# Two units that project queries before values, small tables on ScalarE's DMA queue, and weight preparation spread over more units, in a fused two-layer attention kernel

## The chip, the cores and the metric

The kernel runs on one core of a Trainium2 chip. The metric is the device time of one execution in microseconds (us); a shorter time is better. The core's engines are named PE (TensorE, the matmuls), DVE (VectorE), ACT (ScalarE), POOL (GpSimd) and SP (SyncE, which issues most DMAs here). They run side by side and meet at semaphores only.

## What is computed

Two layers of the same form, one after the other, on x of 8 batches x 512 tokens x 512 features in float32. Layer 0 has 8 heads, layer 1 has 16. Cut from the reference:

```python
xn = _ln(x, ln_w, ln_b)
q = xn @ Wq + bq
k = xn @ Wk + bk + (1.0 - src_mask) * -1000000.0
q = jax.nn.softmax(q.reshape(b, t, h, dh), axis=-1)
k = jax.nn.softmax(k.reshape(b, t, h, dh), axis=1)
v = ((xn @ Wv + bv) * src_mask).reshape(b, t, h, dh)
att = jnp.einsum('bnhd,bnhl->bhdl', k, v)
y = jnp.einsum('bnhd,bhdl->bnhl', q, att).reshape(b, t, d)
emb_out = (jax.nn.silu(emb) @ W_emb + b_emb)[:, None, :]
scale, shift = jnp.split(emb_out, 2, axis=2)
hh = _ln(y, ln2_w, ln2_b) * (1.0 + scale) + shift
hh = jax.nn.silu(hh) @ W_out + b_out
return x + hh
```

So the attention is linear: K^T V is a 512x512 matrix, of which only the blocks of the heads count, and q multiplies it.

## The kernel before

**Units and steps.** A unit is one batch in one layer: units 0 to 7 are layer 0, units 8 to 15 are layer 1. Step u works on three units at once: the projections K, V, Q, the attention matrix (`att_ps`) and Y = q x attention (`attend`) of unit u ("front"); the transposition YT of the normalised Y, the scale-and-shift with silu (h) and the output projection O of unit u-1 ("back"); and the normalisation and transposition XT of unit u+1 ("following"). `step(u, front, back, following)` is written once for each engine; each engine runs its own list, and the lists meet at counting semaphores.

**Precision.** Every float32 operand is split in a high and a low float16 half, and a product is three matmuls (hi x hi, hi x lo, lo x hi; `split_pairs`, `product`, L417). One 128x512 tile of a projection is 12 matmuls. High halves are ACT's (`split_high`, L1031, L1081, L1132, L1063), low halves DVE's (`split_low` L720 for weights, L862 for K, L908 for q) or POOL's (L1182 for v, L1221 for h, L1177 for x).

**Weights.** The halves need a scale by the weight's largest entry. `find_peak` (L677) takes the peak of each row on DVE, PE sums over partitions (`sum_w`, L486), `find_scale` makes the power of two, and `split_high` and `split_low` follow. The order is K, V, Q, O. Layer 0's weights are prepared in the start and unit 0; those of layer 1 in units 1 to 4, one a unit, from the one buffer `w_stage` (`stages`), with the split in the unit behind. `gather_film` and `film_tables` make the scale-and-shift tables of a layer, at the end of unit 0 and in unit 8.

**PSUM.** The tiles of K, YT, V, Q, XT and O share a ring of six banks (Y takes O's). `slot` gives tile i of a stage its bank by its place in `SLOTS`, modulo six: K0 to K3 are in banks 0 to 3, YT0 to YT3 in 4, 5, 0, 1, V0 to V3 in 2, 3, 4, 5, Q0 to Q3 in 0, 1, 2, 3. `take_bank` lets PE wait until the tile that had the bank before, by `order(u)`, has been read; `FREES` names the semaphore: `k_masked` for K (DVE's read L836), `film_read` for YT (ACT's Identity L1102), `v_biased` for V (L894), `q_biased` for Q (L922).

**Order on the engines around the change.** PE in a step: K, YT, V, Q, attention, XT, O, attend. DVE: read K, statistics of the next x, h of blocks 0 and 1, low half of K, h of blocks 2 and 3, read V, peak of a weight (units 1 to 4), then for each tile of Q read, maximum and subtraction (L922, L925, L927), mask of the attention (L934), sums of q (L938), residual (L824), read Y (L964). ACT: normalised Y, exp of K, tanh and Identity of YT blocks 0 and 1 (L1095, L1102), high half of K, blocks 2 and 3, high half of h, of v, next x, exp and high half of q. SP: transposes k's and q's halves by DMA (L335) and issues the loads.

## Time and profile before

| | us |
|---|---|
| median of three runs | 897.56 |
| the three runs | 895.36 to 899.39 |
| the profiled execution | 897.69 |
| its span | 895.9 |

The span is the part of the execution that the hardware profiler covers; 1.8 us lie outside it. The mean clock granted to TensorE is 0.981 of full. The profile's page gives sums over the whole span, and its other views a stretch, an engine or a line. In a timeline a row is one instruction, or several alike in succession with their count; "[2.06 <-DMA ...]" says that the engine stood still for 2.06 us before it, and what ended that. Times start at the span's start. A matmul row's duration overlaps with the next; the distance of the starts is what counts.

### The profile page before, as it was taken

The numbers are of one execution on the slowest core, as the hardware profiler recorded it, in microseconds if no ns is written. First come the engines' busy times: TensorE is split into PE (matmuls) and PEld (weight loads), VectorE is DVE, ScalarE is ACT, GpSimd is POOL, SyncE is SP. The second block draws the span as 40 slices with busy tenths as digits, with TensorE's granted clock in tenths as the row PEclk, the third lists the DMA queues.
The fourth block names the chain that finished last, engine by engine and source line by source line (L and its number), as shares of the span: only waits on it lengthen the run. The fifth ranks groups of instructions, "written<-read, shape, count | busy, mean of one in ns | idle before, by whom it ended". The sixth has DMA issues, their size and how long they took to land.

```text
span 895.9 us, 13969 instructions
## 1 busy us (share of the span) xinstructions
PE 837.4 (93%) x5245; PEld 458.8 (51%) x5245; DVE 721.0 (80%) x1512; ACT 536.2 (60%) x913; POOL 382.2 (43%) x328
## 2 busy tenths in 40 slices
PE   3587999999999999999999899999999999999967
PEld 2236455454555446455554545555554645555544
DVE  5899897898888788787868978687786978687674
ACT  3456484857757594864827467474838567473713
POOL 1053355524545543453544236455534436455402
PEclk9897999999999999999999999999999999999988
DMA  9922135542526455231644224234443325223322
GB/s 317 352 47 49 59 48 108 141 106 44 142 63 142 106 154 141 56 86 60 193 102 95 61 68 110 69 95 106 94 106 92 86 48 112 66 48 95 48 48 94
DMA packets 162420, 90.83 MB, mean 101 GB/s; under 512 B 134673, under 2 KB 134961, under 8 KB 162353
## 3 DMA queue, kind: packets, MB, share of 16 engines
q1 hardware_dynamic: 162352, 89.94, 39.9%
q8 instruction: 41, 0.67, 0.3%
q14 instruction: 27, 0.21, 0.1%
HBM read 39.60 MB, written 16.78 MB: 63 GB/s over the span
## 4 chain that ended last, share of the span: by engine, by line
PE 53%; DVE 20%; issue 9%; ACT 9%; DMA 4%; POOL 4%; SPq 1%; DVEq 0%; POOLq 0%
PE ring L417 45%; PE ring L450 3%; PE att_ps L417 3%; DVE sb_v_or_q L922 2%; DVE sb_q_max L925 2%; DVE sb_kt_or_y L964 2%; DVE sb_y_stats L968 2%; ACT sb_k_or_qt L1073 2%; ACT sb_kq_hi L1081 2%; POOL sb_ht_lo L1221 2%; ACT sb_tanh L1095 1%; ACT sb_xh_or_h L1102 1%; DVE sb_row_peak L677 1%; DVE sb_tanh L908 1%; POOL sb_y_rstd L1172 1%
## 5 line engine op out<-in xcount | busy, mean ns | idle before, releaser
L417 PE MATMUL ring<-sb_w_hi,sb_xt_hi 128*128 128x512 f16 x512 | 194.6, 380 | 4.5 <-DVE sb_k_max L836 2.3
L417 PE MATMUL ring<-sb_w_hi,sb_xt_lo 128*128 128x512 f16 x512 | 194.8, 380 | 0.0
L417 PE MATMUL ring<-sb_w_lo,sb_xt_hi 128*128 128x512 f16 x512 | 194.6, 380 | 0.0
L1068 ACT ACTIVATE sb_kt_or_y<-sb_kt_or_y,sb_y_add,sb_y_rstd 128x512 f32<-128x512 f32 x64 | 46.9, 804 | 169.3 <-DVE sb_y_add L976 169.3
L1221 POOL TENSOR_TENSOR sb_ht_lo<-sb_xh_or_h,sb_ht_hi 128x512 f16<-128x512 f32 x60 | 68.5, 1170 | 114.3 <-ACT sb_ht_hi L1063 114.3
L417 PE MATMUL ring<-sb_xt_hi,sb_w_hi 128*128 128x512 f16 x256 | 97.9, 382 | 7.3 <-DVE sb_xt_lo L1005 7.3
L417 PE MATMUL ring<-sb_xt_lo,sb_w_hi 128*128 128x512 f16 x256 | 97.8, 382 | 0.0
L417 PE MATMUL ring<-sb_xt_hi,sb_w_lo 128*128 128x512 f16 x256 | 97.5, 381 | 0.0
L417 PE MATMUL ring<-sb_w_hi,sb_ht_hi 128*128 128x512 f16 x240 | 91.5, 381 | 5.1 <-ACT sb_xh_or_h L1053 4.4
L417 PE MATMUL ring<-sb_w_lo,sb_ht_hi 128*128 128x512 f16 x240 | 91.4, 381 | 0.0
L417 PE MATMUL ring<-sb_w_hi,sb_ht_lo 128*128 128x512 f16 x240 | 91.2, 380 | 0.0
L1128 ACT ACTIVATE sb_v_or_q<-sb_v_or_q 128x512 f32<-128x512 f32 x64 | 40.4, 631 | 80.1 <-DVE sb_v_or_q L927 80.1
L417 PEld LDWEIGHTS ring<-sb_w_hi,sb_xt_hi 128*128 128x128 f16 x512 | 50.2, 98 | 65.3 <-issue 3.9
L417 PEld LDWEIGHTS ring<-sb_w_hi,sb_xt_lo 128*128 128x128 f16 x512 | 50.2, 98 | 60.7 <-issue 0.6
L1191 POOL TENSOR_TENSOR sb_x<-sb_x,sb_bias_o 128x512 f32<-128x512 f32 x64 | 80.7, 1291 | 0.0
L1177 POOL TENSOR_TENSOR sb_xt_lo<-sb_xh_or_h,sb_xt_hi 128x512 f16<-128x512 f32 x60 | 67.5, 1156 | 30.4 <-ACT sb_xt_hi L1058 30.4
L417 PEld LDWEIGHTS ring<-sb_w_lo,sb_xt_hi 128*128 128x128 f16 x512 | 50.2, 98 | 58.4 <-issue 0.6
L1182 POOL TENSOR_TENSOR sb_v_parts<-sb_v_or_q,sb_v_parts 128x512 f16<-128x512 f32 x64 | 76.8, 1228 | 7.0 <-ACT sb_v_parts L1114 7.0
L1073 ACT ACTIVATE sb_k_or_qt<-sb_k_or_qt,sb_k_shift 128x512 f32<-128x512 f32 x64 | 45.4, 710 | 46.2 <-DVE sb_k_shift L844 46.2
L836 DVE CUSTOM_DVE_ANT_0 sb_k_or_qt<-ring,sb_mask_add,sb_scale_down 128x512 f32<-128x512 f32 x64 | 46.4, 744 | 32.6 <-issue 32.5
L1186 POOL TENSOR_TENSOR sb_att_lo<-sb_att,sb_att_hi 128x512 f16<-128x512 f32 x16 | 18.5, 1158 | 121.1 <-ACT sb_att_hi L1134 121.1
L922 DVE SCALAR_TENSOR_TENSOR sb_v_or_q<-ring,sb_scale_down,sb_bias_q 128x512 f32<-128x512 f32 x64 | 47.6, 744 | 20.9 <-POOL sb_v_parts L1182 20.8
(184 smaller groups left out, 1764.0 us busy)
## 6 DMA issues: line engine op xcount, KB each, us to landing
out<-sb_x SPq DMA_DIRECT2D x15, 1024.0 KB, 5.1
sb_x<-out SPq DMA_DIRECT2D x8, 1024.0 KB, 5.9
sb_x<-in_x SPq DMA_DIRECT2D x7, 1024.0 KB, 10.1
sb_mask_raw<-in_mask SPq DMA_DIRECT2D x16, 256.0 KB, 6.0
sb_w_stage<-in_L_cond_Wk SPq DMA_DIRECT2D x2, 1024.0 KB, 6.9
sb_w_hi<-in_L_cond_W_emb SPq DMA_DIRECT2D x2, 1024.0 KB, 11.7
sb_w_lo<-in_L_cond_W_emb SPq DMA_DIRECT2D x2, 1024.0 KB, 12.5
sb_wemb<-in_L_cond_film_emb_W SPq DMA_DIRECT2D x2, 1024.0 KB, 6.5
```

The costliest lines, as they stand in the source:

```text
L417: last = nc.tensor.matmul(out, lhs, rhs, start=(n == 0), stop=(n == len(pairs) - 1))
L450: last = nc.tensor.transpose(out[:, j * P:j * P + P], source(i, j), ident[:])
L836: nc.vector.tensor_tensor_reduce(k_or_qt[:, i, :], bank("K", i), mask_add[:], scale_down[:, front, K_:K_ + 1], -3.4e38, ALU.add, ALU.max, ...
L922: nc.vector.scalar_tensor_tensor(out=q[:, t, :], in0=bank("Q", t), scalar=scale_down[:, front, Q_:Q_ + 1], in1=bias_q[front][:], op0=ALU.m ...
L1068: nc.scalar.activation(kt_or_y[:, t, :], kt_or_y[:, t, :], ACT.Identity, bias=y_add[:, t:t + 1], scale=y_rstd[:, t:t + 1]).then_inc(yh_rea ...
L1073: nc.scalar.activation(k_or_qt[:, i, :], k_or_qt[:, i, :], ACT.Exp, bias=k_shift[:, i:i + 1], accum_out=k_sum[:, i:i + 1]).then_inc(k_exp, 1)
L1128: nc.scalar.activation(q[:, t, :], q[:, t, :], ACT.Exp).then_inc(q_exp, 1)
L1177: nc.gpsimd.tensor_tensor(xt_lo[:, c, :], xh_or_h[:, c, :], xt_hi[:, c, :], ALU.subtract).then_inc(xt_lo_ready, 1)
L1182: nc.gpsimd.tensor_tensor(v_lo[:, t, :], v[:, t, :], v_hi[:, t, :], ALU.subtract).then_inc(v_lo_ready, 1)
L1186: nc.gpsimd.tensor_tensor(att_lo[:], att[:], att_hi[:], ALU.subtract).then_inc(att_lo_ready, 1)
L1191: nc.gpsimd.tensor_tensor(xt(unit, t), xt(unit, t), bias_o[layer][:], ALU.add).then_inc(x_biased, 1)
L1221: nc.gpsimd.tensor_tensor(lo[:, c, :], xh_or_h[:, c, :], hi[:, c, :], ALU.subtract).then_inc(ht_lo_ready, 1)
```

## The change

Six pieces:

1. `QUERIES_FIRST`: in units 0 and 15 the projection of Q stands in front of V. q then has the buffer `wemb` instead of `v_or_q`. Banks by `slot` stay as they are.
2. The five small tables (column table, identity, embedding, mask, head blocks) are issued by ACT instead of SP. The transposition of the mask on PE and its copy stand behind K's weight preparation.
3. Layer 0's weights are prepared in the order K, Q, V, O (`NTH`). W_v and W_q change buffers.
4. Unit 0: DVE reads and centres all of q in front of k's low half and `v_scales`, and `gather_film`, the peak of W_o and the scales of layer 1's norm stand in front of the reads of Y. XT and the film transposition stand in front of the attention on PE. The halves of W_o are made in unit 1.
5. Layer 1's weights: W_q is loaded in `wemb` between steps 0 and 1, W_k in unit 1 behind k's transposed low half, W_v in unit 3, W_o in unit 4. Peaks stand in units 1 to 4 (K, Q, V, O), scales and high halves in units 2 to 5, low halves in units 3 to 6. The film weights are loaded in units 6 and 7. In unit 8 `gather_film` stands in front of the last read of K, and `film_tables` in front of q.
6. Unit 15: Q, V, then two tiles of O in front of the attention. DVE reads q0 and q1 in front of k's low half, q2 and q3 behind it, and centres all four behind h.

```diff
+QUERIES_FIRST = (0, UNITS - 1)
+NTH = (0, 2, 1, 3)
...
-    here = [(name, i) for name, i in SLOTS if 0 <= u + OFFSET[name] < UNITS]
+    stages = [name for name, _ in STAGES]
+    if u in QUERIES_FIRST:
+        v, q = stages.index("V"), stages.index("Q")
+        stages[v], stages[q] = "Q", "V"
...
-        stages = ((w_stage, kt_or_y, v_parts, w_stage), (w_stage,) * 4)
+        stages = ((w_stage, v_parts, kt_or_y, w_stage), (w_stage, w_stage, wemb, wemb))
...
                 turn(kt_hi, kq_hi[:], k_hi_ready, 4 * (u + 1), kt_hi_ready)
-                if 2 <= u <= 4:
-                    load_w(1, u - 1)
+                if u in (3, 4):
+                    load_w(1, (V_, O_)[u - 3])
                 turn(kt_lo, k_lo, k_lo_ready, 4 * (u + 1), kt_lo_ready)
...
+                if u == 1:
+                    load_w(1, K_)
...
+                if u not in QUERIES_FIRST:
+                    values()
...
                 project_tokens("Q", u, Q_, front, xt_hi, xt_lo, between=with_q)
+                if u in QUERIES_FIRST:
+                    values()
+                if u == 0:
+                    turn_x(u)
+                    turn_film(0)
+                if u == UNITS - 1:
+                    pe.wait_ge(ht_lo_ready, 4 * u)
+                    project_tokens("O", u, O_, back, ht_hi, ht_lo, (0, 1))
...
                 if u_is_first:
+                    split_low(0, V_)
+                    x_affine(u + 1)
+                    for t in range(T):
+                        read_q(t)
+                        centre_q(t)
                     split_k()
+                    v_scales(0)
...
+                        if c == 2 and u == UNITS - 1:
+                            read_q(0)
+                            read_q(1)
                         if c == 2 and front is not None:
                             split_k()
+                        if c == 2 and u == UNITS - 1:
+                            read_q(2)
+                            read_q(3)
...
                 if u_is_first:
                     gather_film(0)
+                    find_peak(0, O_)
+                    ln_scales(1)
...
+                if u == 1:
+                    split_high(0, O_)
...
-                    elif u == B:
-                        gather_film(1)
+                    elif u == B:
+                        film_tables(1)
+                        output_scale(1)
...
+            act.dma_start(cols[:], cols_d).then_inc(cols_loaded, 16)
+            act.dma_start(ident[:], ident_d).then_inc(ident_loaded, 16)
+            act.dma_start(emb, emb_d).then_inc(emb_loaded, 16)
+            act.dma_start(mask_rows, mask0_d.rearrange("b (t p) -> (b t) p", p=P)).then_inc(mask_rows_loaded, 16)
+            act.dma_start(blocks[:], blocks_d).then_inc(tables_loaded, 16)
```

**PE, unit 15, from the YT transposes on.** L450 and L461 are the transposes, L417 and L428 the matmuls of a product; ring0 to ring5 are the six banks. Before, then after:

```order
L450 MATMUL ring0<-sb_ident,sb_kt_or_y 128x128 [waits k_masked]
L450 MATMUL ring0<-sb_ident,sb_kt_or_y 128x128 x3
L450 MATMUL ring1<-sb_ident,sb_kt_or_y 128x128 [waits k_masked]
L450 MATMUL ring1<-sb_ident,sb_kt_or_y 128x128 x3
L417 MATMUL ring2<-sb_w_hi4,sb_xt_hi 128x512 [waits k_masked]
```

```order
L461 MATMUL ring0<-sb_ident,sb_kt_or_y 128x128 [waits k_masked]
L461 MATMUL ring0<-sb_ident,sb_kt_or_y 128x128 x3
L461 MATMUL ring1<-sb_ident,sb_kt_or_y 128x128 [waits k_masked]
L461 MATMUL ring1<-sb_ident,sb_kt_or_y 128x128 x3
L428 MATMUL ring0<-sb_w_hi4,sb_xt_hi 128x512 [waits film_read]
```

The first projection behind the transposes has moved from bank 2 (V0, where K2 was) to bank 0 (Q0, where YT2 is), and its wait from DVE's read of K to ACT's read of YT.

**DVE, unit 15, from the reciprocal of k's sums on.** L882 and L961 are h, L862 and L885 k's low half, L894 and L892 the reads of V, L922 and L902 the reads of Q, L925 and L907 the maximum, L927 and L909 the subtraction. Before, then after:

```order
L851 RECIPROCAL sb_k_recip<-sb_k_sum 128x4 [waits k_sum_scaled]
L882 SCALAR_TENSOR_TENSOR sb_xh_or_h<-sb_tanh,sb_xh_or_h 128x512 [waits film_read] x2
L862 SCALAR_TENSOR_TENSOR sb_k_or_qt<-sb_k_or_qt,sb_k_recip,sb_kq_hi 128x512 [waits k_hi_ready,k_recip_ready]
L862 SCALAR_TENSOR_TENSOR sb_k_or_qt<-sb_k_or_qt,sb_k_recip,sb_kq_hi 128x512 [waits k_lo_ready,k_hi_ready] x3
L882 SCALAR_TENSOR_TENSOR sb_xh_or_h<-sb_tanh,sb_xh_or_h 128x512 [waits film_read] x2
L894 SCALAR_TENSOR_TENSOR sb_v_or_q<-ring,sb_scale_down,sb_bias_v 128x512 [waits pe_V] x4
L922 SCALAR_TENSOR_TENSOR sb_v_or_q<-ring,sb_scale_down,sb_bias_q 128x512 [waits pe_Q,v_lo_ready]
```

```order
L872 RECIPROCAL sb_k_recip<-sb_k_sum 128x4 [waits k_sum_scaled]
L961 SCALAR_TENSOR_TENSOR sb_xh_or_h<-sb_tanh,sb_xh_or_h 128x512 [waits film_read] x2
L902 SCALAR_TENSOR_TENSOR sb_wemb<-ring,sb_scale_down,sb_bias_q 128x512 [waits pe_Q] x2
L885 SCALAR_TENSOR_TENSOR sb_k_or_qt<-sb_k_or_qt,sb_k_recip,sb_kq_hi 128x512 [waits k_hi_ready,k_recip_ready]
L885 SCALAR_TENSOR_TENSOR sb_k_or_qt<-sb_k_or_qt,sb_k_recip,sb_kq_hi 128x512 [waits k_lo_ready,k_hi_ready] x3
L902 SCALAR_TENSOR_TENSOR sb_wemb<-ring,sb_scale_down,sb_bias_q 128x512 [waits pe_Q] x2
L961 SCALAR_TENSOR_TENSOR sb_xh_or_h<-sb_tanh,sb_xh_or_h 128x512 [waits film_read] x2
L907 TENSOR_REDUCE sb_q_max<-sb_wemb 128x16 [waits q_biased]
```

The reads of Q have moved in front of and right behind k's low half, and no longer wait for v's low half; the reads of V stand behind the centring of q.

**SP, from q's transposes of unit 0 into unit 1.** L335 and L350 are the DMA transposes, L311 and L326 the loads of weights, L302 and L314 the load of the next mask. Before, then after:

```order
L335 DMA_TRANSPOSE sb_k_or_qt<-sb_tanh 128x16x128 [waits q_lo_ready]
L311 DMA sb_w_stage<-in_L_cond_Wk 128x4x512 [waits w_ready0]
L302 DMA sb_mask_raw<-in_mask 128x512 [waits mask_ready]
L335 DMA_TRANSPOSE sb_kt_or_y<-sb_kq_hi 128x16x128 [waits pe_YT,k_hi_ready]
L335 DMA_TRANSPOSE sb_kt_or_y<-sb_k_or_qt 128x16x128 [waits k_lo_ready]
```

```order
L350 DMA_TRANSPOSE sb_k_or_qt<-sb_tanh 128x16x128 [waits q_lo_ready]
L326 DMA sb_wemb<-in_L_cond_Wq 128x4x512 [waits q_lo_ready,q_summed]
L314 DMA sb_mask_raw<-in_mask 128x512 [waits mask_ready]
L350 DMA_TRANSPOSE sb_kt_or_y<-sb_kq_hi 128x16x128 [waits pe_YT,k_hi_ready]
L350 DMA_TRANSPOSE sb_kt_or_y<-sb_k_or_qt 128x16x128 [waits k_lo_ready]
L326 DMA sb_w_stage<-in_L_cond_Wk 128x4x512 [waits w_ready0]
```

The load of layer 1's W_k has moved from in front of unit 1's transposes to behind them; W_q of layer 1 has its old place.

## Rows read from the trace of the kernel before

**Rows 1.** The page, busy time of each engine over the whole span

```profile
PE 837.4 (93%) x5245; PEld 458.8 (51%) x5245; DVE 721.0 (80%) x1512; ACT 536.2 (60%) x913; POOL 382.2 (43%) x328
```

**Rows 2.** Timeline of PE, first attend product, units 0, 1, 2, 4; start, duration

```profile
84.79 0.26 PE L417 MATMUL ring<-sb_att_hi,sb_k_or_qt 128*128 128x128 f16 x1 [5.37 <-DMA sb_k_or_qt<-sb_tanh]
...
142.22 0.22 PE L417 MATMUL ring<-sb_att_hi,sb_k_or_qt 128*128 128x128 f16 x1 [0.89 <-issue]
...
195.46 0.22 PE L417 MATMUL ring<-sb_att_hi,sb_k_or_qt 128*128 128x128 f16 x1 [0.36 <-issue]
...
300.25 0.22 PE L417 MATMUL ring<-sb_att_hi,sb_k_or_qt 128*128 128x128 f16 x1 [0.40 <-issue]
```

**Rows 3.** Timeline of PE, start of the attention products, units 10 and 11

```profile
597.27 0.89 PE L417 MATMUL att_ps<-sb_kt_or_y,sb_v_parts 128*128 128x128 f16 x13
...
647.58 0.61 PE L417 MATMUL att_ps<-sb_kt_or_y,sb_v_parts 128*128 128x128 f16 x8
```

**Rows 4.** Line 311 between 8 and 9 us, the load of W_v

```profile
L311 SPq DMA_DIRECT2D sb_kt_or_y<-in_L_cond_Wv x1: 650/650/650, 8.4 to 8.4; - x1
...
DMA to landing us min/median/max: 11.8/11.8/11.8
```

**Rows 5.** Timeline of DVE, the start: peak of W_v

```profile
21.02 2.28 DVE L677 TENSOR_REDUCE sb_row_peak<-sb_kt_or_y 128x4 f32<-128x2048 f32 x1
```

**Rows 6.** Timeline of PE, unit 0: first matmuls of K, first of V

```profile
29.18 0.61 PE L417 MATMUL ring<-sb_xt_hi,sb_w_hi 128*128 128x512 f16 x1 [7.34 <-DVE sb_xt_lo L1005]
29.58 0.63 PE L417 MATMUL ring<-sb_xt_lo,sb_w_hi 128*128 128x512 f16 x1
...
44.19 0.38 PE L417 MATMUL ring<-sb_w_hi,sb_xt_hi 128*128 128x512 f16 x1 [2.31 <-DVE sb_k_max L836]
```

**Rows 7.** Timeline of DVE: reads of Y, low half of W_o, read of K

```profile
86.84 1.39 DVE L964 TENSOR_TENSOR sb_kt_or_y<-ring,sb_q_recip 128x512 f32<-128x512 f32 x2
...
99.21 2.08 DVE L720 SCALAR_TENSOR_TENSOR sb_w_lo<-sb_w_stage,sb_scale_up,sb_w_hi 128x512 f16<-128x512 f32 x3
...
101.96 0.74 DVE L836 CUSTOM_DVE_ANT_0 sb_k_or_qt<-ring,sb_mask_add,sb_scale_down 128x512 f32<-128x512 f32 x1
```

**Rows 8.** Timeline of SP, unit 1: transposition of k's low half

```profile
114.91 3.32 SPq L335 DMA_TRANSPOSE sb_kt_or_y<-sb_k_or_qt  x1
```

**Rows 9.** Line 311 between 166 and 168 us, a load beside a transposition

```profile
DMA to landing us min/median/max: 6.9/6.9/6.9
```

**Rows 10.** Timeline of DVE: first read of q in units 1, 2, 5; unit 2's peak

```profile
122.38 0.75 DVE L922 SCALAR_TENSOR_TENSOR sb_v_or_q<-ring,sb_scale_down,sb_bias_q 128x512 f32<-128x512 f32 x1
...
173.60 2.29 DVE L677 TENSOR_REDUCE sb_row_peak<-sb_w_stage 128x4 f32<-128x2048 f32 x1 [2.06 <-DMA sb_w_stage<-in_L_cond_Wv]
...
177.43 0.75 DVE L922 SCALAR_TENSOR_TENSOR sb_v_or_q<-ring,sb_scale_down,sb_bias_q 128x512 f32<-128x512 f32 x1
...
331.83 0.75 DVE L922 SCALAR_TENSOR_TENSOR sb_v_or_q<-ring,sb_scale_down,sb_bias_q 128x512 f32<-128x512 f32 x1 [2.25 <-POOL sb_v_parts L1182]
```

**Rows 11.** Timeline of PE, unit 8: first attend product

```profile
512.80 0.23 PE L417 MATMUL ring<-sb_att_hi,sb_k_or_qt 128*128 128x128 f16 x1 [1.45 <-DVE sb_x L824]
```

**Rows 12.** Timeline of PE, unit 15: V, attention, attend

```profile
828.28 0.38 PE L417 MATMUL ring<-sb_w_hi,sb_xt_hi 128*128 128x512 f16 x1
...
849.00 1.17 PE L417 MATMUL att_ps<-sb_kt_or_y,sb_v_parts 128*128 128x128 f16 x18
...
863.46 0.26 PE L417 MATMUL ring<-sb_att_hi,sb_k_or_qt 128*128 128x128 f16 x1 [3.85 <-DMA sb_k_or_qt<-sb_tanh]
```

**Rows 13.** Timeline of ACT, unit 15: Identity of YT block 2

```profile
836.53 0.77 ACT L1102 ACTIVATE sb_xh_or_h<-ring,sb_film_now 128x512 f32<-128x512 f32 x1
```

**Rows 14.** Timeline of POOL, unit 15: low half of v

```profile
843.68 4.94 POOL L1182 TENSOR_TENSOR sb_v_parts<-sb_v_or_q,sb_v_parts 128x512 f16<-128x512 f32 x4
```

**Rows 15.** Timeline of DVE, unit 15: sums of q, residuals, first read of Y

```profile
857.11 2.46 DVE L938 TENSOR_REDUCE sb_q_sum<-sb_v_or_q 128x16 f32<-128x512 f32 x4
...
860.36 1.97 DVE L824 SCALAR_TENSOR_TENSOR sb_x<-ring,sb_down_o,sb_x 128x512 f32<-128x512 f32 x3
...
865.00 0.69 DVE L964 TENSOR_TENSOR sb_kt_or_y<-ring,sb_q_recip 128x512 f32<-128x512 f32 x1 [2.67 <-PE ring L417]
```

More of the change, by code:

```diff
@@ L499, in sum_ln @@
                 for layer in range(LAYERS):
-                    last = nc.tensor.matmul(sums[0][:, 8 + layer:9 + layer], ones[:], peak[:, layer, LN:LN + 1], start=True, stop=True)
+                    last = nc.tensor.matmul(sums(0, 8 + layer), ones[:], peak[:, layer, LN:LN + 1], start=True, stop=True)
                 last.then_inc(ln_summed, 1)
@@ new lines, in step, with read_q @@
+                q = queries(u)
+                if front is not None:
+                    by_head = lambda a: a.rearrange("p (h e) -> p h e", h=heads)
+                    wide = lambda a: a.unsqueeze(2).broadcast_to([P, heads, D // heads])
+                def read_q(t):
+                    dve.wait_ge(done["Q"], 4 * u + t + 1)
+                    nc.vector.scalar_tensor_tensor(out=q[:, t, :], in0=bank("Q", t), scalar=scale_down[:, front, Q_:Q_ + 1],
+                                                   in1=bias_q[front][:], op0=ALU.mult, op1=ALU.add).then_inc(q_biased, 1)
@@ L1105, in step, with split_v @@
                         high(c)
-                if front is not None:
+                q = queries(u)
+                def split_v():
                     if front == 0:
```

282 lines of the change are left out of this document (151 added, 131 removed).

## Prediction, made before the changed kernel was run

> **What bounds the kernel now.** I read the page first. TensorE is busy 93% of the span [rows 1], so only its gaps, and its stretches at a lowered clock, can move the end. The next view is the timeline of TensorE at the same point of every unit. Between units 10 and 11 the attention products lie 50.31 us apart (647.58 - 597.27) with nothing but matmuls between them [rows 3]: that is the dense unit. The first attend products of units 0, 1, 2 and 4 lie farther apart: 142.22 - 84.79 = 57.4, then 53.24, then 104.79 for two units [rows 2]. So the slack is at both ends: the start until unit 4 (the units 2 to 4 alone are 53.24 + 104.79 - 3 x 50.31 = 7.1 over dense; the weights of layer 1 are measured there), unit 8, and the last unit with the chain behind it. The timelines of VectorE, ScalarE, GpSimd and SyncE at those places say what TensorE waits for.
>
> **Start, part by part.** K of unit 0 starts at 29.18, behind VectorE [rows 6]. VectorE is occupied in one piece from 21.02: peak of W_v, low half of W_k, low half of x^T [rows 5], 8.16 us. The change puts W_q there in place of W_v. Its two V-only steps go (0.4), and VectorE reaches it earlier, because the wait for the mask transposition is gone; then the landing of W_q decides. W_v, second in the queue, was issued at 8.42 and landed 11.8 later, at 20.2 [rows 4]. W_q takes this place with five small issues gone ahead of it; the DMA engines are full all this time, so I gain little of them: 19.9. K starts at 19.9 + 7.8 = 27.7, 1.5 earlier (bounds: 0, were W_q late, to 3).
>
> Here the Trainium skill has a rule that speaks against part of the change: "DMA: Bandwidth & Descriptors", section "Issuing engines are not separate DMA queues", says that transfers issued from ScalarE and SyncE share the same 16 engines, so a second issuing engine brings no bandwidth. The trace of before has one issuing engine only and can't show it; 11.8 us for 1 MB agrees with engines that are full. By the rule the tables' move gives only the issue time on SyncE; were it wrong, W_q would land up to 2 us sooner.
>
> The wait of 2.31 in front of V [rows 6] goes: before, the reads of K, whose bank V takes, stood on VectorE behind v_scales; this stands after q now, and the reads begin at 36. That makes 3.8 us by the time of attention in unit 0, and attend starts earlier still, near 77 to 79 against 84.79, since q is centred before attention. But behind attend VectorE now has gather_film, the peak of W_o (2.28 and 0.3 of small steps, by the peak in [rows 5]) and the scales of the second layer norm (1.3) ahead of the reads of Y. I walk VectorE through its new order with the old durations: the reads of K end at 41, q is read and centred until 56, k's low half stands at 59.5, v's scales at 62.1, v is read until 64.8. GpSimd's low half of v ends 4.6 behind that read, as before; so attention products at 69.4, sums of q done 76.1, gather_film until 81, peak 83.6, scales 84.9. Y is read at 84.9 instead of 86.84 [rows 7]. From there to the read of K of unit 1 at 101.96 stand the same steps less the low half of W_o, 4 x 0.69 = 2.7 [rows 7], plus its scale, 0.9. So K of unit 1 is read at 98.3; with 0.3 for meeting GpSimd, 98.6, **3.4 earlier** (0.5 to 5).
>
> **Unit 1.** The low half of W_o moves behind k_recip, where VectorE waits for ScalarE anyway: 0.3. Before, K^T's low half was issued at 114.91, 12.95 after K was read, and took SyncE 3.32 [rows 8]. Now it is issued at 98.6 + 12.95 + 0.3 = 111.85 and done at 115.2. W_k of layer 1 is loaded only behind it; before, it was in place long before it was needed. Such a load landed, beside a transposition, in 6.9 [rows 9]. With no other transfer in flight I take 0.8 less, an estimate between 5 and 6.9; so 121.3. Its peak stands in VectorE's order ahead of the first read of Q, takes 2.6, and puts that read at 123.9 instead of 122.38 [rows 10]. What is queued behind this wait is all of q, and attend waits for that. In unit 2 attend came 195.46 - 177.43 = 18.0 after the same read [rows 2, 10]. So attend of unit 1 starts at 141.95, against 142.22: of 3.4 us **0.3 are left** (with the landing and K's read at their ends, -2.5 to +2).
>
> **Units 2 to 4.** Unit 2 now measures W_q, loaded long before into wemb: no wait of 2.06 [rows 10], and the peak nearly fits in the 2.25 that VectorE waits there for v's low half in an undisturbed unit [rows 10]. So 50.4 instead of 53.24. Unit 3 has W_v instead of W_q, whose steps from the peak on take 177.43 - 173.60 = 3.83 on VectorE [rows 10] against 2.6: 1.25 lost; unit 4 has W_o as before. Together **1.6 gained** (0 to 3). The high and low halves, now a unit later, stand where ScalarE and VectorE wait; film loads had no wait before and have none now: 0.
>
> **Unit 8.** Film tables stood between the residuals, and attend waited 1.45 for them [rows 11]. They now stand ahead of q, in place of gather_film, which stands ahead of the last read of K. **1.5 gained** (0 to 3: nothing if the gather makes K late, twice the stall if the clock and q gain too).
>
> **Unit 15.** This is the term that decides. Before, V follows the YT transposes at once, at 828.28, since its bank 2 was K's and long read [rows 12]. Q first means bank 0, and bank 0 is YT2's. ScalarE frees it with the Identity of feature block 2, which starts at 836.53 and takes 0.77 [rows 13], behind the high halves of K. Nothing of the change makes this earlier. So TensorE stands still from 828.28 to 837.3, 9.0 us, and restarts at half clock: in unit 0, after 7.34 of standing still, nine matmuls went at a distance of 0.40 to 0.43 [rows 6], where V's and Q's 96 took 849.00 - 828.28 = 20.7 [rows 12], 0.216 each. That is 1.9 more. Q ends at 849.6, V at 860.0. Two output tiles fill 860.0 to 865.2. V's low half on GpSimd took 4.94 for four [rows 14]; it starts at 861.1, after ScalarE's exp and high halves of q, and ends at 866.0. Attention products 2.9: 868.9; masking 0.7; sums of q 2.46 and 0.8 [rows 15]: 872.9; three residuals 1.97 [rows 15]: Y is read from 874.9 instead of 865.00 [rows 15]. Before, TensorE entered attend after 3.85 of standing still [rows 12] and VectorE waited a further 0.5 between two Y; that is gone. 874.9 - 865.0 - 0.5: **9.4 lost** (6 to 11). Behind it the chain to the end is the same.
>
> **Sum.** -0.3 - 1.6 - 1.5 + 9.4 = +6.0. The profiled execution took 897.69 with a span of 895.9; 897.69 + 6.0 = 903.7. The median of 897.56 is 0.1 below the profiled one, so this isn't corrected. A difference under 0.5%, 4.5 us, can't be told from none for this kernel: its bounds are 893.1 and 902.05.
>
> **Rivals.**
> The tail costs TensorE's own work only (0.24; work as above, but v's low half is ready when V and the output tiles end, for ScalarE is through with q early). Then O and attention end at 870.8, Y is read from 871.5, and 6.0 is lost. Against it speaks that high halves of q stand ahead of v on ScalarE. 897.69 - 3.4 + 6.0 = 900.3. To it belongs that attend of unit 1 keeps the 3.4 us (W_k lands before v's low half is ready): 897.69 - 6.5 + 9.4 = 900.6.
>
> Faster (0.08): the bank of YT2 is free early, or Q starts on another bank. It decides if Q starts within 3 us of 828.28. Then q's transposes are landed long before attend, the wait of 3.85 goes, and 3.4 + 3.85 are gained: 890.4. For it: early q is what the wait of 3.85 asks for. Against it: the timeline of ScalarE.
>
> Start worse (0.16): the order of unit 0 on VectorE meets GpSimd's work, W_k lands at 6.9 or later, and the gather makes K of unit 8 late. No gain of 3.4 and up to 1.5 lost, tail 9.3 to 10.5: 907 to 909.
>
> The start's tables change nothing (within my own case, 0.52): K starts at 29.18; this takes 1.5 from the read of K, and 905.
>
> **How the numbers follow.** The likeliest, 0.52, gives 903.7, with its own range 901 to 906; a fourth of it lies under 902.05. Same: 0.12 of it, 0.21 of the first rival, 0.02 beside: 0.35. Slower: 0.40, 0.15 and 0.02: 0.57. Faster: 0.08. The range of 898 to 909 leaves out the fast rival, and about 0.08 of others.
>
> **What would show it.** Right: TensorE idle some 9 us in front of Q of unit 15, ended by the Identity on ScalarE; a lowered clock after it; v's low half as the releaser of attention there; Y read 9 to 10 us later, counted from the YT transposes. W_k's load as the releaser of VectorE's peak in unit 1. The wait ahead of V in unit 0 gone, attend of unit 2 some 50.4 behind that of unit 1, no wait of attend for x in unit 8. Wrong: Q of unit 15 close behind the transposes; or unit 1's first attend earlier than 140.

## The result, and the profile after

The changed kernel is slower: a median of 908.03 us in four executions (907.64 to 908.43), against 898.47 for the kernel before in its four (895.36 to 899.5). The ratio is 1.0112, with a 95% interval of 1.0085 to 1.0138. The forecast was 903.7 with a range of 898 to 909, so the direction and the range held and the size was missed by 4.3 us. The time lies outside the 901 to 906 that the likeliest case had for itself. The profiled execution took 907.77, its span 906.0, and its mean granted clock is 0.977 of full (0.981 before).

The page of the kernel after, busy time of each engine (against [rows 1]):

```profile
PE 842.1 (93%) x5245; PEld 460.9 (51%) x5245; DVE 718.2 (79%) x1510; ACT 536.2 (59%) x915; POOL 386.1 (43%) x328
```

No engine has less or more to do in any way that matters: the same 5245 matmuls, and VectorE 2.8 us less busy. TensorE's span grew by 10.1: 4.7 of it is busy time (842.1 against 837.4 for the same matmuls, at a lower mean clock), and 5.4 is gaps (63.9 against 58.5). The waits of TensorE, grouped by what ended them (us in total, times, longest), show the new ones:

```profile
PE ring L428 <- ACT sb_xh_or_h L1151: 8.9, 1, 8.9
...
PE att_ps L428 <- POOL sb_v_parts L1260: 4.1, 2, 2.2
PE ring L428 <- DVE sb_wemb L902: 3.1, 1, 3.1
PE ring L428 <- POOL sb_att_lo L1264: 2.9, 1, 2.9
...
PE ring L428 <- DVE sb_x L841: 2.1, 1, 2.1
```

The first is the bank of YT2 in unit 15; the second and fourth stand at the attention of units 0 and 15; the third is V's first tile in unit 0, behind a read of Q; the last is attend of unit 15, behind the residuals.

**The start.** Timelines of VectorE, TensorE and GpSimd, unit 0 of the kernel after, in order of time:

```profile
18.62 2.29 DVE L699 TENSOR_REDUCE sb_row_peak<-sb_kt_or_y 128x4 f32<-128x2048 f32 x1 [0.40 <-DMA sb_kt_or_y<-in_L_cond_Wq]
...
26.40 0.61 PE L428 MATMUL ring<-sb_xt_hi,sb_w_hi 128*128 128x512 f16 x1 [4.50 <-DVE sb_xt_lo L1051]
...
43.84 4.75 DVE L742 SCALAR_TENSOR_TENSOR sb_w_lo<-sb_v_parts,sb_scale_up,sb_w_hi 128x512 f16<-128x512 f32 x4
...
44.65 6.30 POOL L1269 TENSOR_TENSOR sb_x<-sb_x,sb_bias_o 128x512 f32<-128x512 f32 x4
...
54.76 0.58 PE L428 MATMUL ring<-sb_w_hi,sb_xt_hi 128*128 128x512 f16 x1 [3.09 <-DVE sb_wemb L902]
...
66.70 5.85 POOL L1260 TENSOR_TENSOR sb_v_parts<-sb_v_or_q,sb_v_parts 128x512 f16<-128x512 f32 x4 [15.76 <-ACT sb_v_parts L1165]
...
67.63 5.47 DVE L914 SCALAR_TENSOR_TENSOR sb_tanh<-sb_wemb,sb_kq_hi 128x512 f16<-128x512 f32 x4
...
72.81 5.28 PE L428 MATMUL att_ps<-sb_v_parts,sb_kt_or_y 128*128 128x128 f16 x48 [1.94 <-POOL sb_v_parts L1260]
...
78.12 0.69 DVE L930 TENSOR_TENSOR sb_att<-att_ps,sb_blocks 128x512 f32<-128x512 f32 x1 [5.03 <-PE att_ps L428]
```

Two rows of the kernel before, on VectorE and TensorE, stand against these:

```profile
49.36 6.72 DVE L862 SCALAR_TENSOR_TENSOR sb_k_or_qt<-sb_k_or_qt,sb_k_recip,sb_kq_hi 128x512 f16<-128x512 f32 x4 [0.86 <-ACT sb_kq_hi L1081]
...
73.13 2.84 PE L417 MATMUL att_ps<-sb_v_parts,sb_kt_or_y 128*128 128x128 f16 x48
```

K starts 2.8 earlier than before (26.40 against 29.18 [rows 6]), but the attention only 0.3 earlier (72.81 against 73.13). In between, low halves on VectorE and work on GpSimd stand side by side twice and both are slow, and V waits for Q. Before had one such meeting too: k's low half took 6.72 beside GpSimd's 6.30 for x and its bias, and takes 3.31 in after, where GpSimd is idle. The attention itself then takes 5.28 where the same 48 matmuls took 2.84. Y of unit 0 is read at 87.60, behind 86.84 of before [rows 7], and K of unit 1 at 100.66, against 101.96.

**Unit 1.** SyncE's queue, VectorE's peak of W_k, and the first product of attend (against 142.22 in [rows 2]):

```profile
114.39 3.06 SPq L350 DMA_TRANSPOSE sb_kt_or_y<-sb_k_or_qt  x1
117.51 0.58 SPq L326 DMA_DIRECT2D sb_w_stage<-in_L_cond_Wk  x1
...
123.47 2.29 DVE L699 TENSOR_REDUCE sb_row_peak<-sb_w_stage 128x4 f32<-128x2048 f32 x1 [4.69 <-DMA sb_w_stage<-in_L_cond_Wk]
...
145.41 0.22 PE L428 MATMUL ring<-sb_att_hi,sb_k_or_qt 128*128 128x128 f16 x1 [1.67 <-issue]
```

Attend of unit 1 is 3.2 later than before, behind a load for which VectorE stands still 4.69 us.

**Unit 15.** Timelines of TensorE, GpSimd and VectorE (against [rows 12, 14, 15]):

```profile
826.01 1.91 PE L461 MATMUL ring<-sb_ident,sb_kt_or_y 128*128 128x128 f32 x16
836.83 0.61 PE L428 MATMUL ring<-sb_w_hi,sb_xt_hi 128*128 128x512 f16 x1 [8.91 <-ACT sb_xh_or_h L1151]
...
859.75 5.37 DVE L914 SCALAR_TENSOR_TENSOR sb_tanh<-sb_wemb,sb_kq_hi 128x512 f16<-128x512 f32 x4
...
860.05 6.08 POOL L1260 TENSOR_TENSOR sb_v_parts<-sb_v_or_q,sb_v_parts 128x512 f16<-128x512 f32 x4 [6.52 <-ACT sb_v_parts L1171]
...
866.41 4.47 PE L428 MATMUL att_ps<-sb_kt_or_y,sb_v_parts 128*128 128x128 f16 x48 [2.19 <-POOL sb_v_parts L1260]
...
875.58 0.22 PE L428 MATMUL ring<-sb_att_hi,sb_k_or_qt 128*128 128x128 f16 x1 [2.10 <-DVE sb_x L841]
...
876.66 1.28 DVE L1011 TENSOR_TENSOR sb_kt_or_y<-ring,sb_q_recip 128x512 f32<-128x512 f32 x2
```

From the YT transposes to the first read of Y it takes 876.66 - 826.01 = 50.65; before, it took 38.47 (its transposes start at 826.53, just ahead of [rows 12]). That distance is the measure of unit 15 in all runs below. A stretch's table, for the attention products of units 15 and 0 (us, PE busy, granted clock, DMA share, GB/s), shows why they are long: 0.50 of full, the 1.2 GHz level, for all of unit 0's and the later part of unit 15's.

```profile
868.00:870.00 2.00, 2.00 (x22) 0.50 0.51 94
72.80:78.10 5.30, 5.28 (x48) 0.50 0.52 99
```

### The profile page after: what moved, and what is told of

Its sections match the earlier page's. It is cut to its first block, busy times and chain, and to the rows that moved or that the text cites. A ratio compares the mean times of both kernels' runs of the same rounds, so it can differ in the third digit from the quotient of the medians.

```text
span 906.0 us, 13953 instructions
## 1 busy us (share of the span) xinstructions
PE 842.1 (93%) x5245; PEld 460.9 (51%) x5245; DVE 718.2 (79%) x1510; ACT 536.2 (59%) x915; POOL 386.1 (43%) x328
## 4 chain that ended last, share of the span: by engine, by line
PE 59%; DVE 18%; issue 7%; ACT 7%; DMA 4%; POOL 3%; SPq 1%; DVEq 0%; POOLq 0%; ACTq 0%
PE ring L428 50%; PE att_ps L428 4%; PE ring L461 3%; DVE sb_q_max L907 2%; DVE sb_v_or_q L902 2%; DMA sb_kt_or_y<-in_L_cond_Wq 2%; DVE sb_row_peak L699 2%; DVE sb_w_lo L742 1%; ACT sb_k_or_qt L1122 1%; POOL sb_v_parts L1260 1%; ACT sb_kq_hi L1130 1%; DVE sb_kt_or_y L1011 1%; ACT sb_tanh L1144 1%; DVE sb_y_stats L1015 1%; ACT sb_xh_or_h L1151 1%
## 5 line engine op out<-in xcount | busy, mean ns | idle before, releaser
L428 PE MATMUL ring<-sb_w_hi,sb_xt_hi 128*128 128x512 f16 x512 | 195.9, 383 | 12.0 <-ACT sb_xh_or_h L1151 8.9
L428 PE MATMUL ring<-sb_w_lo,sb_xt_hi 128*128 128x512 f16 x512 | 195.7, 382 | 0.0
L428 PE MATMUL ring<-sb_w_hi,sb_xt_lo 128*128 128x512 f16 x512 | 195.6, 382 | 0.0
L428 PE MATMUL ring<-sb_xt_hi,sb_w_hi 128*128 128x512 f16 x256 | 98.0, 383 | 4.7 <-DVE sb_xt_lo L1051 4.5
L428 PE MATMUL ring<-sb_xt_lo,sb_w_hi 128*128 128x512 f16 x256 | 97.8, 382 | 0.0
L428 PE MATMUL ring<-sb_xt_hi,sb_w_lo 128*128 128x512 f16 x256 | 97.8, 382 | 0.0
L428 PE MATMUL ring<-sb_w_hi,sb_ht_hi 128*128 128x512 f16 x240 | 91.0, 379 | 7.2 <-ACT sb_xh_or_h L1100 4.5
L428 PE MATMUL ring<-sb_w_lo,sb_ht_hi 128*128 128x512 f16 x240 | 91.0, 379 | 0.0
L428 PE MATMUL ring<-sb_w_hi,sb_ht_lo 128*128 128x512 f16 x240 | 91.0, 379 | 0.0
L1260 POOL TENSOR_TENSOR sb_v_parts<-sb_v_or_q,sb_v_parts 128x512 f16<-128x512 f32 x64 | 79.3, 1270 | 22.3 <-ACT sb_v_parts L1165 15.8
L428 PEld LDWEIGHTS ring<-sb_w_hi,sb_xt_hi 128*128 128x128 f16 x512 | 50.5, 99 | 72.9 <-ACT sb_xh_or_h L1151 9.1
L428 PEld LDWEIGHTS ring<-sb_w_hi,sb_xt_lo 128*128 128x128 f16 x512 | 50.4, 99 | 61.6 <-issue 2.1
L428 PEld LDWEIGHTS ring<-sb_w_lo,sb_xt_hi 128*128 128x128 f16 x512 | 50.5, 99 | 59.4 <-issue 1.7
L1176 ACT ACTIVATE sb_v_or_q<-sb_v_or_q 128x512 f32<-128x512 f32 x56 | 35.4, 632 | 70.0 <-DVE sb_v_or_q L909 70.0
L961 DVE SCALAR_TENSOR_TENSOR sb_xh_or_h<-sb_tanh,sb_xh_or_h 128x512 f32<-128x512 f32 x64 | 45.4, 724 | 20.3 <-ACT sb_xh_or_h L1151 20.2
```

The costliest lines, as they stand in the source:

```text
L428: last = nc.tensor.matmul(out, lhs, rhs, start=(n == 0), stop=(n == len(pairs) - 1))
L961: nc.vector.scalar_tensor_tensor(out=xh_or_h[:, c, :], in0=tanh[:, c % 2, :], scalar=1.0, in1=xh_or_h[:, c, :], op0=ALU.add, op1=ALU.mult) ...
L1176: nc.scalar.activation(q[:, t, :], q[:, t, :], ACT.Exp).then_inc(q_exp, 1)
L1260: nc.gpsimd.tensor_tensor(v_lo[:, t, :], v[:, t, :], v_hi[:, t, :], ALU.subtract).then_inc(v_lo_ready, 1)
```

## The experiments

All times are medians, with the ratio to the kernel before as run on the same chip (its medians there: 897.31 for the first four, 898.83 for the next three and the first of "Together", 898.68 for the rest). "After" is the changed kernel, 908.03. Where two runs stem from different chips, their ratios are compared, and a difference of about 0.1% between them isn't clear of noise.

### Which part loses: unit 15 in its old order

```diff
-QUERIES_FIRST = (0, UNITS - 1)
+QUERIES_FIRST = (0,)
```

and with it the places of the two output tiles, of the reads of Q and of ACT's q and v in unit 15, as before.

> The changed kernel, with unit 15 in its old order (K, YT, V, Q, attention, O) on all engines; everything else of the change stays. Theory (the loss is unit 15's): the 8.9 us of TensorE in front of Q and what follows it go, attend of unit 15 falls from 875.6 to about 863.2, and the time is 908.0 - 10.4 = 897.6, the kernel before's within 1 us. Rival (part of the loss is the start: W_k of layer 1 late, q's low halves beside GpSimd): over 901.

Measured: 896.34 (894.84 to 899.6), ratio 0.9989, 0.9973 to 1.0006. YT to Y takes 38.50 again. The whole loss, 11.7 us against after, is unit 15's; the rest of the change together is worth about nothing.

### Is it the bank: Q of unit 15 in V's banks

```diff
 def slot(name, i, u=None):
+    if u in OTHER_BANKS:            # (UNITS - 1,)
+        name = {"V": "Q", "Q": "V"}.get(name, name)
     return 3 if name == "O'" else slot("O", i) if name == "Y" else SLOTS.index((name, i)) % RING
```

The order of the work is that of after. Only the banks differ in unit 15: Q takes 2 to 5, V takes 0 to 3.

> The changed kernel with Q first in unit 15, but Q in banks 2, 3, 4, 5 and V in 0, 1, 2, 3 of the ring in that unit, so that Q0's bank is K2's, long read. Theory (the bank of YT2 is what Q waits for): TensorE has no gap of 8.9 behind the YT transposes, Q starts within 1 us of them, and v's low half ends near 856.5 instead of 866.1; VectorE reads Y near 867.5 instead of 876.7; 908.0 - 9 = 899. Rival 1 (early q saves the wait of 3.85 ahead of attend, once the bank is free): 893 or less. Rival 2 (Q waits for something else too): the gap stays, 907 to 908.

Measured: 898.65 (896.95 to 901.76), ratio 1.0012, 0.9995 to 1.0028. The 8.9 us are gone, and TensorE runs through. The profiled execution was the longest of the ten, 901.76, so distances within the unit are compared here, not times from the start. Its timeline from the transposes on, GpSimd's low half of v, and the attention:

```profile
829.06 1.91 PE L466 MATMUL ring<-sb_ident,sb_kt_or_y 128*128 128x128 f32 x16
830.81 0.38 PE L433 MATMUL ring<-sb_w_hi,sb_xt_hi 128*128 128x512 f16 x1
...
854.12 6.06 POOL L1265 TENSOR_TENSOR sb_v_parts<-sb_v_or_q,sb_v_parts 128x512 f16<-128x512 f32 x4 [6.52 <-ACT sb_v_parts L1176]
...
860.43 4.47 PE L433 MATMUL att_ps<-sb_kt_or_y,sb_v_parts 128*128 128x128 f16 x48 [2.18 <-POOL sb_v_parts L1265]
...
869.59 0.22 PE L433 MATMUL ring<-sb_att_hi,sb_k_or_qt 128*128 128x128 f16 x1 [2.10 <-DVE sb_x L846]
```

YT to Y takes 870.67 - 829.06 = 41.61: 9.0 less than after, but 3.1 more than in the old order. So the bank explains most of the loss, and the rival "faster" had its mechanism right and its price wrong. With Q in time, v is what comes late: its low half, then a half-clock attention, then the sums of q and the residuals, for which attend still waits 2.10.

### Unit 1: W_k loaded ahead of k's transposes

```diff
+                if u == 1:
+                    load_w(1, K_)
                 turn(kt_hi, kq_hi[:], k_hi_ready, 4 * (u + 1), kt_hi_ready)
...
-                if u == 1:
-                    load_w(1, K_)
```

> The changed kernel with the load of layer 1's W_k in unit 1 in front of k's transposed high half instead of behind the low half. Theory (the load's landing holds q of unit 1): issued near 110, landed near 116, VectorE's wait of 4.69 ahead of the peak is gone, q is first read at 121.5 instead of 126.1, attend of unit 1 starts near 141 instead of 145.4, and all units behind keep it: 908.0 - 4.5 = 903.5. Rival (the two transpositions get slower beside the load and attention waits for them, or ScalarE holds q): 1.5 or less gained, 906.5 or more.

Measured: 904.49 (902.95 to 905.17), ratio 1.007, 1.0046 to 1.0094; 3.5 less than after. VectorE's first read of q stands at 121.38 instead of 126.07, and attend at

```profile
141.38 0.22 PE L428 MATMUL ring<-sb_att_hi,sb_k_or_qt 128*128 128x128 f16 x1 [1.04 <-issue]
```

instead of 145.41. The load behind the low half costs these 4.0 us, of which 3.4 are left at the YT transposes of unit 15 (822.57 against 826.01).

### Unit 0: V and Q with swapped banks

The edit of the second experiment, for unit 0 instead of unit 15.

> The changed kernel with V and Q in each other's banks in unit 0 alone, so that V0 doesn't wait for the read of Q2. Theory (VectorE's order bounds unit 0, TensorE's wait of 3.09 is covered): the wait goes, attention starts under 1 us earlier than 72.8, K of unit 1 is read under 1 us earlier than 100.7: 907.0 to 908.0, the same as the changed kernel. Rival (V's late start is what makes v's low half and attention late): the 3.09 and 1.5 of half clock come back, attention at 68.5, and 904 to 905.

Measured: 909.84 (908.26 to 910.1), ratio 1.0129, 1.0108 to 1.015. The 3.09 in front of V are gone and no time is won; the 1.8 more than after aren't clear of noise (the intervals overlap), though the forecast was at most 908. TensorE arrives early and then waits: 1.83 for a read of v in front of XT, 0.77 for the film's pick, and 4.20 for GpSimd in front of the attention, which starts at 73.76:

```profile
65.18 1.31 PE L466 MATMUL ring<-sb_ident,sb_xh_or_h 128*128 128x128 f32 x8 [1.83 <-DVE sb_v_or_q L897]
67.14 6.37 POOL L1265 TENSOR_TENSOR sb_v_parts<-sb_v_or_q,sb_v_parts 128x512 f16<-128x512 f32 x4 [15.75 <-ACT sb_v_parts L1170]
```

So unit 0 is bounded by the order on VectorE and GpSimd, not by this wait. (XT's wait for v's reads, 0.41 in after, grows with the swap, so the run doesn't test a unit 0 without any wait for a bank.) A wait that tops the list needn't be the one that counts.

### The sums of q ahead of the mask

In after, VectorE stands idle 5.0 and 5.8 us in front of the masking of the attention, and sums q behind it. In units 0 and 15:

```diff
                     for t in range(T):
                         low_q(t)
+                    sum_q()
                     mask_att()
-                    sum_q()
```

> The changed kernel with the sums of q and their reciprocal (3.25 us on VectorE) in front of the mask of the attention instead of behind it, in units 0 and 15. VectorE stands still there for 5.0 and 5.8 us until the attention products end. Theory (behind these products the end waits for VectorE's order): in unit 15 the residuals start at 871.6 instead of 874.8, attend's wait of 2.1 for x goes, Y is read near 874, 2.6 earlier; in unit 0 the reads of Y move by 3.2, K of unit 1 with them, and the load of W_k too, so 2.5 to 3 are kept: 908.0 - 5.5 = 902.5. Rival (W_k or another transfer swallows unit 0's part): 905.5. Rival 2 (TensorE and GpSimd's half of the attention are the bound): 907 to 908.

Measured: 904.18 (903.11 to 905.4), ratio 1.0068, 1.0049 to 1.0088. YT to Y takes 48.08, 2.6 less, and attend of unit 1 comes at 143.04, 2.4 earlier. That is between the theory (902.5) and its rival (905.5). And 1.6 of the tail's 2.6 is the clock: here the attention of unit 15 took 2.84 behind a wait of 2.16, where after had 4.47 behind 2.19.

### The sums also ahead of q's low half

```diff
+                    dve.wait_ge(q_exp, 4 * (u + 1))
+                    sum_q()
                     for t in range(T):
                         low_q(t)
-                    sum_q()
                     mask_att()
```

The sums read one operand, the low halves two. So VectorE has one-operand work while GpSimd makes v's low half.

> As the run with the sums early, but the sums of q stand in front of q's low halves too. The low halves (5.4 us for four beside GpSimd's low half of v, 2.75 alone) then meet v's low half only at its end. Theory (both engines slow each other when both read two operands): v's low half takes 5.0 to 5.4 instead of 5.9 to 6.1, attention of unit 15 starts 0.8 earlier, the low halves take 3 to 4; but q's transposed low half is issued 2 later, near 867, and attend of unit 15 starts near 873.5: within 1 us of the run with the sums early, 902 to 903.5. Rival (the two don't meet): v's low half stays at 6, and the later transposition makes it 904 or more.

Measured: 901.67 (899.75 to 903.21), ratio 1.0033, 1.002 to 1.0047. Timelines of VectorE, GpSimd and TensorE, unit 15:

```profile
857.90 2.46 DVE L920 TENSOR_REDUCE sb_q_sum<-sb_wemb 128x16 f32<-128x512 f32 x4
...
858.20 4.49 POOL L1261 TENSOR_TENSOR sb_v_parts<-sb_v_or_q,sb_v_parts 128x512 f16<-128x512 f32 x4 [6.53 <-ACT sb_v_parts L1172]
...
862.14 2.91 DVE L914 SCALAR_TENSOR_TENSOR sb_tanh<-sb_wemb,sb_kq_hi 128x512 f16<-128x512 f32 x4
...
862.95 2.84 PE L428 MATMUL att_ps<-sb_kt_or_y,sb_v_parts 128*128 128x128 f16 x48 [0.58 <-POOL sb_v_parts L1261]
```

The same four GpSimd instructions take 4.49 instead of 6.08, the same four on VectorE 2.91 instead of 5.37. Nothing differs but what stands beside them: the slowness in after is the meeting of the two. Attend now waits for the transposition of q's low half (1.12) and no longer for the residuals. YT to Y is 46.41.

### The kernel before, with the tables and unit 8's film alone

The five small loads move from SP to ACT, and in unit 8 `gather_film` and `film_tables` take the places that after gives them. The mask's transposition and everything else stay as before.

```diff
-            sp.dma_start(ident[:], ident_d).then_inc(ident_loaded, 16)
...
+            act.dma_start(cols[:], cols_d).then_inc(cols_loaded, 16)
+            act.dma_start(ident[:], ident_d).then_inc(ident_loaded, 16)
...
+                        if u == B and i == C - 1:
+                            gather_film(1)
```

> The kernel before with two parts of the change alone: the five small tables issued by ScalarE, and unit 8's film work moved (gather in front of the last read of K, tables in front of q). Units 0 and 15, and all weights, in their old order. Theory (tables: SyncE's issue time and W_v's landing; film: a stall of 1.45): K of unit 0 starts near 27.5 instead of 29.2, but the reads of K there still stand behind v_scales, and attention waits for the same chain on VectorE, so 1.5 of it arrives at unit 1; unit 8's attend has no wait for x: 897.3 - 3 = 894.5. Rival (both are hidden): 897.3. The mask's transposition stays in front here, so that the start may gain nothing: then 895.8.

Measured: 894.37 (890.54 to 897.53), ratio 0.9952, 0.9935 to 0.9968. TensorE at K's and V's first tile of unit 0, and attend of unit 1:

```profile
26.85 0.61 PE L411 MATMUL ring<-sb_xt_hi,sb_w_hi 128*128 128x512 f16 x1 [6.62 <-DVE sb_xt_lo L999]
41.99 0.38 PE L411 MATMUL ring<-sb_w_hi,sb_xt_hi 128*128 128x512 f16 x1 [2.31 <-DVE sb_k_max L832]
...
140.22 0.22 PE L411 MATMUL ring<-sb_att_hi,sb_k_or_qt 128*128 128x128 f16 x1 [1.13 <-issue]
```

K starts nearly as early as in after, V's wait of 2.31 is still there, and K of unit 1 is read at 99.71, 0.9 earlier than in after. So the tables alone bring most of the earlier start. From K's start to the read of K of unit 1 it takes 72.9, as before (72.8), against 74.3 in after: queries first in unit 0, with what was moved along with it there, loses 1.5. The profiled execution is the shortest of the ten, 3.8 under the median. Part of that lies in the tail: the last attend ran at full clock and took 2.6, where before's took 5.2 at 0.50.

### The tables back on SP

On the kernel of the first experiment, the five loads go back to SP, to the places that before gives them.

> The changed kernel with unit 15 in its old order and the five tables issued by SyncE again, in their old places. Theory (the start's gain is the tables'): the scales of the norm wait for the column table and embedding again, W_q lands later, K of unit 0 starts at 27.5 to 29 instead of 26.4, and unit 1 follows: 896.3 + 2 = 898.3. Rival (the reordered preparation made the gain, the mask's transposition being gone from the front): K starts at 26.5 to 27 and 896.3 to 896.8.

Measured: 897.76 (896.49 to 901.36), ratio 0.9997, 0.9983 to 1.0012. With the tables on ACT the ratio was 0.9989, and the two intervals overlap, so the medians alone don't show a gain. SyncE's issue of W_q with the tables on ACT (the first experiment) and here, then VectorE's peak of W_q and the first matmul of K here:

```profile
4.20 1.34 SPq L326 DMA_DIRECT2D sb_kt_or_y<-in_L_cond_Wq  x1
...
8.08 0.46 SPq L326 DMA_DIRECT2D sb_kt_or_y<-in_L_cond_Wq  x1
...
19.82 2.29 DVE L700 TENSOR_REDUCE sb_row_peak<-sb_kt_or_y 128x4 f32<-128x2048 f32 x1 [1.66 <-DMA sb_kt_or_y<-in_L_cond_Wq]
...
27.60 0.61 PE L434 MATMUL ring<-sb_xt_hi,sb_w_hi 128*128 128x512 f16 x1 [4.23 <-DVE sb_xt_lo L1043]
```

With the tables on ACT the same peak started at 18.39, and K at 26.16: W_q was issued 3.9 sooner and landed 1.4 sooner. In all the runs with the start of after, K starts between 25.99 and 27.07, so the move is worth 0.5 to 1.6 us at K's start. The new order of the preparation brings something by itself too: K starts at 27.60 here against 29.18 before, with the tables on SP in both.

### Together, unit 15 in the old order

The first and third experiments, and in unit 0 the sums of q, the peak of W_o and the scales of layer 1's norm ahead of the mask.

> The changed kernel with unit 15 in its old order, W_k's load in front of k's transposes in unit 1, and in unit 0 the sums of q, the peak of W_o and the scales of layer 1's norm in front of the mask of the attention. Theory (the three losses add up): 896.3 by the run with unit 15 undone, less 3.5 to 4 for W_k, less 3 to 5 for VectorE's 5 us of standing still in unit 0: 888 to 890, about 1% below the kernel before. Rival (what unit 0 gains is taken back by TensorE's half clock or the film tables before unit 1): 892 to 893.

Measured: 888.71 (888.46 to 890.87), ratio 0.9897, 0.9878 to 0.9916. Attend of unit 1 comes at 137.36.

The same with `sum_q` ahead of `low_q` in unit 0:

> The merged kernel (unit 15 in its old order, W_k early, peak of W_o and scales of the norm ahead of the mask) with the sums of q also ahead of q's low halves in unit 0. Theory (low halves of q and of v slow each other): v's low half from about 5.6 to 4.6, attention of unit 0 starts 0.5 to 1 earlier, and K of unit 1 with it: 888.0. Rival (unit 0 is held by the peak of W_o in front of the mask): the same 888.7.

Measured: 889.12 (888.66 to 889.64), ratio 0.9895, 0.988 to 0.991: no difference in the time. In the profiled executions there is one until the tail: attention of unit 0 starts at 71.55 instead of 72.96, though masking then waits for the peak of W_o and the scales of the norm, which end at 77.56; attend of unit 1 comes at 136.42 instead of 137.36, and the YT transposes of unit 15 at 817.43 instead of 818.51. The last attend then takes 5.2 at 0.50 of the clock, where the other's took 4.3, and the spans are 886.8 and 886.9. So 1.1 was won in unit 0 and most of it was lost again to the clock at the end.

### Queries first in unit 15 after all

The kernel just above, but with unit 15 as in after, Q and V in swapped banks there, and the sums ahead of q's low half.

> The same, but unit 15 in the change's order with Q first, with Q and V in each other's banks, and the sums ahead of q's low halves there too. From the YT transposes to the first read of Y: 38.5 us in the old order, 50.7 in the changed kernel, 41.6 with other banks, 46.4 with the sums first. Theory (both gains add up): 41.6 - 4.2 = 37.4, 1 us less than in the old order, 887.0. Rival (with the bank free, v's low half is the bound, and the sums can't help since VectorE reads v late): 40 to 41, 890 to 891.

Measured: 886.11 (885.4 to 887.68), ratio 0.9864, 0.9846 to 0.9882: the fastest kernel of the study, 1.4% under the kernel before. The start of attend of unit 15 in the kernel just above and here, and the first read of Y here:

```profile
854.39 0.27 PE L428 MATMUL ring<-sb_att_hi,sb_k_or_qt 128*128 128x128 f16 x1 [3.88 <-DMA sb_k_or_qt<-sb_tanh]
...
853.18 0.22 PE L433 MATMUL ring<-sb_att_hi,sb_k_or_qt 128*128 128x128 f16 x1 [0.50 <-DMA sb_k_or_qt<-sb_tanh]
...
854.12 1.29 DVE L1018 TENSOR_TENSOR sb_kt_or_y<-ring,sb_q_recip 128x512 f32<-128x512 f32 x2 [0.65 <-PE ring L433]
```

The YT transposes start at 816.98, so it takes 37.14, 1.4 less than the 38.50 of the old order. The four reads of Y then follow each other in 3.0 us (854.12 to 857.12), where with Q last they need 3.8 (855.93 to 859.70). Attend waits 0.50 for the transposed q instead of 3.88, and runs at full clock, 2.8 us, instead of 5.2 at 0.50. Projecting queries first in the last unit is a gain of 3.0 us (886.11 against 889.12), once it has banks that are free and an order on VectorE that meets GpSimd less (v's low half takes 4.95). The clock is a good part of it: the old order too can have its last attend at full clock (2.6 in the seventh experiment), and from the first read of Y to the end it then took 29.3, against 29.6 here and 30.9 in the kernel just above.

## Why the prediction was right, and where it was off

**Unit 15 (right, slightly under).** TensorE's standstill was forecast at 9.0 and measured 8.91, ended by ScalarE's Identity as said; the restart at half clock is there, shorter than forecast (six matmuls 0.40 to 0.43 apart, 836.83 to 839.36, some 1.3 lost, where nine and 1.9 were forecast); v's low half on GpSimd releases the attention. The term was +9.4. Measured, the YT transposes stand 0.5 earlier than before and the end 10.1 later, so it is 10.6. Two sizes were off. The attention was put at 2.9 and took 4.47, its clock falling to 0.50 on the way; why isn't settled (below). GpSimd's low half was put at the 4.94 of [rows 14] and took 6.08, since VectorE's low halves of q now stand beside it. Against this, 1.6 came back in the reads of Y and behind, where 0.5 was forecast. Undoing this unit alone gives all of the loss back, and other banks alone 9.4 of it.

**The start (the step that failed).** K's start was forecast at 27.7 and was 26.40, 1.3 better, since W_q had landed at 18.6 and not at 19.9. Yet K of unit 1 was forecast at 98.6 and was read at 100.66. The walk of VectorE "with the old durations" is what failed, for a duration holds only beside the same work on GpSimd. 2.0 us are lost at W_v's low half (4.75 instead of the 2.7 of four such), q is centred at 58.08 instead of 56, and q's low halves, 5.47 instead of 2.7, and v's on GpSimd, 5.85 instead of 4.6, meet. Then attention runs at half clock, 2.4 more. The 0.3 taken "for meeting GpSimd" had no row behind it. Attention was forecast at 69.4 and started at 72.81. Chance gave part of it back. `gather_film` was walked with its old 4.9 and took 2.3 (81.77 to 84.02): before, four of its small steps took 1.08 to 1.11 each (81.64 to 86.10) beside GpSimd's low half of x (81.56 to 86.05), and in after they take 0.18 to 0.19 and are over as GpSimd starts (82.74). So the old durations had a meeting in them that went, while two others came; the prediction looked for neither. The wait of 2.31 in front of V went, as said, but V now waits 3.09 for the read of Q2, whose bank V0 takes; the prediction looked for this in unit 15 and not in unit 0. By the fourth experiment, taking this wait away wins nothing. Of the 3.4 us forecast, 1.3 were there.

**Unit 1 (mechanism right, under).** The load behind the low half does hold VectorE, its landing was forecast at 6.1 behind the transposition and took 5.9, and moving it gives 3.5 us. Attend was put 18.0 behind the first read of q, by a row of unit 2. Unit 1's own rows of before gave 142.22 - 122.38 = 19.8 [rows 2, 10], and 19.3 was measured. With the 2.1 from the start this makes +3.2 instead of -0.3, 3.5 of the 4.1 us by which the profiled execution missed. Unit 15 adds 1.2, and units 2 to 4 and 8 take 0.5 off.

**Units 2 to 4 and unit 8 (right).** From attend of unit 1 to that of unit 4 it takes 301.54 - 145.41 = 156.1, against 158.0 before: 1.9 gained, 1.6 forecast. Unit 8's attend no longer waits for x:

```profile
511.17 0.22 PE L428 MATMUL ring<-sb_att_hi,sb_k_or_qt 128*128 128x128 f16 x1 [0.39 <-issue]
```

After was 1.4 behind at unit 5 (352.08 against 350.65) and is 0.3 ahead at unit 9 (561.47 against 561.77): 1.7 gained, 1.5 forecast.

**The rivals.** That the tail costs TensorE's own work only (900.3) fell: GpSimd released the attention. "Faster" fell for after, and its price of 893 or less fell with the second experiment; its mechanism, another bank and then no wait of 3.85 for the transposed q, is real and pays in the last kernel. "Start worse" (0.16) has the measured time in its 907 to 909, and one of its reasons held, VectorE's meeting with GpSimd; counted from its issue W_k landed no later than forecast, and the gather did K of unit 8 no harm. The likeliest case gave 901 to 906. So the range held by what it left room for, not by the main sum. That the tables change nothing fell: K starts 0.5 to 1.6 sooner for them.

**The tables on a second issuing engine.** By the Trainium skill, "DMA: Bandwidth & Descriptors", section "Issuing engines are not separate DMA queues", a second issuing engine brings no bandwidth. The runs agree. With the tables on ACT, SyncE issued W_q 3.9 us sooner (4.20 against 8.08), but it took 14.2 from issue to landing instead of 11.7, so that VectorE's peak started only 1.4 sooner (18.39 against 19.82). What the earlier issue won, the longer landing mostly took back. The sum had counted on a landing at 19.9, 0.3 sooner than W_v's before; in after it came at 18.6.

**What stays open.** Whether queries first in unit 0, with all that was mended later, beats values first there wasn't run. A unit 15 with other banks in which the sums don't move wasn't run in the last kernel either. And why a standstill of 2.19 left the attention of unit 15 at half clock in after, and one of 2.16 left it at full clock with the sums early, isn't settled.

## What to carry to other kernels

When a stage is moved ahead of another, look up which buffer of a shared ring it now inherits and who frees that, in every unit where it moves: the wrong bank cost 9 us here. With the right bank alone the new order was still behind the old one (898.65 against 896.34); with q's sums moved too it was 3.0 ahead. When you walk an engine through a new order, old durations hold only if its new neighbours on the other engine are the same; look also for meetings that the old durations already hold, and price a two-operand step on VectorE beside GpSimd at nearly the sum of both (a pair took 1.56 us here, 1.80 one after the other). And a load that nobody waited for, moved behind something, has to be followed to its next reader, in that reader's own unit.
